# Second mamba layer: first half batch loaded during the 1-bit layer before it, the residual's moments taken between the scans

## The reference, cut to what matters

```python
# second 1-bit layer
x = x + linear_bit(silu(linear_bit(x_n, w1, g1)) * linear_bit(x_n, w2, g2), w3, g3)
# second mamba layer: hidden_states = ctx_1024 (4, 512, 256), z = layernorm(x)
xi = einsum('bld,ed->bel', hidden_states, in_proj_w)          # (4, 512, 512)
u = silu(conv1d(xi, conv_w, 4 taps, per channel) + conv_b)
dt_low, B, C = split(einsum('bdl,ed->bel', u, x_proj_w))      # 16 + 16 + 16 rows
delta = softplus(dt_low @ dt_proj_w + dt_proj_b)
A = -exp(A_log)                                               # (512, 16)
state_t = exp(delta_t * A) * state_(t-1) + delta_t * u_t * B_t
y_t = sum over the 16 states of state_t * C_t
x = x + swap((y + D * u) * silu(z))
```

## Time and profile before

| | us |
|---|---|
| median of 3 runs | 4210.7 (4209.96 to 4212.67) |
| the profiled execution | 4212.01 |
| its span | 4210.3 |

### The profile page before, as it was taken

One profiled execution on the slowest core, in us unless ns is written; L12 is line 12 of the kernel. 1 busy time (PEld: TensorE's weight loads), 2 busy tenths in 40 slices (PEclk: granted clock), 3 DMA queues, 4 the chain that ended last, 5 costly groups with the idle time before them and its releaser, 6 DMA issues. The chain is left out here.

```text
span 4210.3 us, 47286 instructions
## 1 busy us (share of the span) xinstructions
PE 3635.0 (86%) x15355; PEld 1743.4 (41%) x15355; DVE 2959.2 (70%) x4185; ACT 1801.8 (43%) x3009; POOL 1463.2 (35%) x1046
## 2 busy tenths in 40 slices
PE   6889865999999999898999879785876888689898
PEld 2333333555555555542333344333332333244454
DVE  3999988578777884457888266527667999834663
ACT  3655541222222221243777453327664655421244
POOL 1889854122211220063000100004436999800122
PEclk8999987999999999997999989896998999989999
DMA  3455441122233212266774110001005555412420
GB/s 104 128 149 141 128 136 54 49 85 69 80 100 100 80 32 72 114 152 97 78 78 47 53 60 0 3 9 64 0 0 141 139 137 138 131 39 70 79 55 22
DMA packets 249834, 338.37 MB, mean 80 GB/s; under 512 B 45602, under 2 KB 147522, under 8 KB 248036
## 3 DMA queue, kind: packets, MB, share of 16 engines
q1 hardware_dynamic: 249620, 335.70, 32.1%
HBM read 284.38 MB, written 53.35 MB: 80 GB/s over the span
## 5 line engine op out<-in xcount | busy, mean ns | idle before, releaser
L727 ACT ACTIVATE m_dA<-m_delta,m_a_neg 128x512 f32<-128x512 f32 x512 | 349.8, 690 | 411.1 <-DVE m_H_bank L806 344.2
L566 PE MATMUL m_y<-m_H,ident 128*128 128x512 f32 x512 | 283.3, 641 | 150.0 <-DVE m_H L823 149.6
L1913 DVE TENSOR_REDUCE a_core_minus_max<-a_core_a 128x1 f32<-128x512 f32 x512 | 317.1, 684 | 59.9 <-PE a_core_a L1739 59.9
L747 POOL TENSOR_TENSOR m_dB<-m_du,m_BC 128x1024 f32<-128x1024 f32 x128 | 302.0, 2360 | 123.0 <-DVE m_du L786 84.5
L736 POOL TENSOR_TENSOR m_H<-m_H,m_BC 128x512 f32<-128x512 f32 x240 | 306.7, 1278 | 95.8 <-DVE m_H L815 95.4
L747 POOL TENSOR_TENSOR XN<-m_du,m_BC 128x1024 f32<-128x1024 f32 x128 | 305.9, 2390 | 2.6 <-DMA m_BC<-bc_ready 2.6
L1865 ACT ACTIVATE X<-a_core_s 128x512 f32<-128x512 f32 x512 | 264.6, 603 | 95.3 <-PE a_core_s L1739 95.2
L1305 POOL TENSOR_TENSOR ctxT<-ctxT,f_scales 128x1024 f32<-128x1024 f32 x48 | 107.0, 2229 | 532.3 <-DVE ctxT L1130 532.3
L574 PE MATMUL m_y<-m_H,ident 128*128 128x512 f32 x512 | 268.4, 612 | 12.0 <-POOL m_H L736 11.9
L1265 ACT ACTIVATE XN<-f_g,f_power_back 128x512 f32<-128x512 f32 x128 | 88.0, 687 | 404.3 <-PE f_g L1202 404.3
L1371 DVE SCALAR_TENSOR_TENSOR XN<-f_u,f_power_back,XN 128x512 f32<-128x512 f32 x128 | 95.8, 748 | 227.9 <-PE f_u L1202 227.9
(11 more groups left out here) (416 smaller groups left out, 8461.5 us busy)
## 6 DMA issues: line engine op xcount, KB each, us to landing
m_BC<-bc_rows SPq DMA_DIRECT2D x224, 512.0 KB, 4.8
XN<-in_L_ffn_w_dram SPq DMA_DIRECT2D x72, 256.0 KB, 2.7
m_BC<-bc_ready SPq DMA_DIRECT2D x32, 512.0 KB, 4.8
ternary<-ctxT SPq DMA_DIRECT2D x96, 128.0 KB, 1.7
a_core_q<-a_q_parts SPq DMA_DIRECT2D x48, 256.0 KB, 12.8
a_core_k<-a_k_parts SPq DMA_DIRECT2D x48, 256.0 KB, 14.8
f_w_tern<-ternary SPq DMA_DIRECT2D x24, 512.0 KB, 6.0
f_core_q<-f_q_parts SPq DMA_DIRECT2D x24, 512.0 KB, 7.9
```

Of the source, the lines that this page charges most:

```text
L566: pe.matmul(ps_y[:, 0, :], ident[:], HD[n % NH], start=False, stop=True, skip_group_check=True).then_inc(s_ad, 1)
L727: act.activation(dA[:, i % NA, :], delta[b % 2][:, e, :], ACT.Exp, scale=a_neg[:, e, k % N:k % N + 1]).then_inc(s_dA, 1)
L747: pool.tensor_tensor(dB[n % ND][:], du[b % 2][:, h * EH:(h + 1) * EH, :], BC[n % NS][:, 0:1, :].broadcast_to([P, EH, L]), ALU.mult).then_i ...
L1913: dve.tensor_reduce(mx[u % 2][:, qt, h:h + 1], ps_a[:, at % NR, 0:n], AX.X, ALU.max, negate=True).then_inc(s_red, 1)
```

## The change

- A new class `FirstHalf` holds delta and du of the first half batch, the first B row and A_log in tiles of their own, allocated before the 1-bit layer, and loads them in that layer's token loop, right behind the issue of the third gain row.
- The second mamba layer's SP queue now begins with BC 0 to 3 and u, then the five small transfers, the weight rows, BC 4 and the second halves. ScalarE waits for the early transfers (`s_half`) instead of the small ones. GpSimd takes the first B row from the early tile. VectorE's wait for the small transfers, and what follows it up to the raised counts, stay as they are.
- The 16 statistics go to steps 4 to 11, two to a step, the aggregates to step 12, root and inverse to step 13, the first batch's gates to steps 15 and 17. The tap diagonals go to steps 1 to 4.
- delta and du become tiles by half. The projection weights are loaded into a part of XN, and the ternary slots lie where xqT comes later, which makes the room.

```diff
+        elif spare is not None:
+            self.in_rows = spare[:, 1:3, :].rearrange("p t (two c) -> p (t two) c", two=2)
+            self.x_rows, self.dt_rows = spare[0:self.W, 0, :], sb("dt_rows", [P, self.EB, self.R])
...
+class FirstHalf:
+    def __init__(self, chip, name, st, parked, bc_parked, a_log, half):
+        self.parked, self.bc_parked, self.a_log, self.half = parked, bc_parked, a_log, half
+        self.delta, self.du = (chip.sb(f"{name}_early_{n}", [P, half, L], F32, st) for n in ("delta", "du"))
+        self.B = chip.sb(name + "_early_B", [P, 1, L], F32, st)
+        self.a_in = chip.sb(name + "_early_a", [P, 2 * half, a_log.shape[1]], F32, st)
+        self.s_half = chip.sem(name + "_early")
+    def load(self, sp):
+        sp.dma_start(self.a_in[:], self.a_log.rearrange("(e p) c -> p e c", p=P)).then_inc(self.s_half, 16)
+        for i, out in ((1, self.delta), (2, self.du)):
+            sp.dma_start(out[:], self.parked[i][:, 0:self.half, :]).then_inc(self.s_half, 16)
+        sp.dma_start(self.B[:], self.bc_parked[0:1].rearrange("(o n) t -> n o t", o=1).broadcast_to([P, 1, L])
+                     ).then_inc(self.s_half, 16)
...
-        ROOT, INVERSE = 5, 7
+        DIAGONAL, MOMENT, ROOT, INVERSE, GATES = 1, 4, 13, 13, (15, 17)
...
-        DIAGONALS = {(0, 3 + e): e for e in range(EB)} if given else ...
+        DIAGONALS = {(0, DIAGONAL + e): e for e in range(EB)} if given else ...
...
             if given:
+                for k in range(NS - 1):
+                    rows_of(0, k)
+                sp.dma_start(u[0][:, 0:EH, :], parked[0][:, 0:EH, :]).then_inc(s_gu, 16)
                 weights.load_small(sp)
-                for i in (2, 1):
-                    park_or_load(i, 0)
-                for k in range(2):
-                    rows_of(0, k)
-                park_or_load(0, 0)
                 weights.load_rows(sp)
-                for k in range(2, NS):
-                    rows_of(0, k)
-                for i in (2, 1, 0):
-                    park_or_load(i, 1)
+                rows_of(0, NS - 1)
+                for out, i in ((du, 2), (delta, 1)):
+                    sp.dma_start(out[0][1][:], parked[i][:, EH:EB, :]).then_inc(s_given, 16)
+                sp.dma_start(u[0][:, EH:EB, :], parked[0][:, EH:EB, :]).then_inc(s_gu, 16)
...
-            act.wait_ge(weights.s_small, weights.SMALL)
+            if given:
+                act.wait_ge(given.s_half, 64)
+            else:
+                act.wait_ge(weights.s_small, weights.SMALL)
...
-                    if k in SILU:
-                        gates(b, SILU.index(k))
+                    if k in (GATES if b < FIRST else SILU):
+                        gates(b, (GATES if b < FIRST else SILU).index(k))
...
                     pool.wait_ge(s_du, b * EB + (h + 1) * EH)
                     if b < FIRST and k % N == 0:
-                        pool.wait_ge(s_given[h], 32)
-                    pool.wait_ge(s_bc[n % NS], 16 * (n // NS + 1))
+                        pool.wait_ge(s_given if h else given.s_half, 32 if h else 64)
+                    if n >= FIRST:
+                        pool.wait_ge(s_bc[n % NS], 16 * (n // NS + 1))
...
+                    row = given.B[:] if n < FIRST else BC[n % NS][:, 0:1, :]
...
             dve.wait_ge(s_pad, 2)
-            norm.moments(dve)
+            if given:
+                norm.begin(dve)
+            else:
+                norm.moments(dve)
...
-                    if given and b == 0 and k == INVERSE:
+                    if b < FIRST and MOMENT <= k < MOMENT + NT // 2:
+                        norm.moment(dve, 2 * (k - MOMENT))
+                        norm.moment(dve, 2 * (k - MOMENT) + 1)
+                    if b < FIRST and k == MOMENT + NT // 2:
+                        norm.aggregate(dve)
+                    if b < FIRST and k == INVERSE:
                         norm.inverse(dve)
...
-        tern = [sb(f"tern{n}", [P, 4, 512], BF16) for n in range(SLOTS)]
+        flat = [at[:].rearrange("p t k n -> p (t k n)") for at in xqT]
+        tern = [at[:, i * 2048:(i + 1) * 2048].rearrange("p (j k) -> p j k", j=4) for at in flat for i in range(4)]
+        tern += [sb(f"tern{n}", [P, 4, 512], BF16)[:] for n in range(len(tern), SLOTS)]
...
             if gains:
                 sp.dma_start(g3, gains[2].rearrange("(o n) -> o n", o=1).broadcast_to([P, F])).then_inc(s_g3, 16)
+            ahead(sp)
+            if gains:
                 sp.wait_ge(s_g3, 16)
...
         with ExitStack() as held:
-            chip.run(stage_mamba, "m3", bc, ScanWeights(chip, "m3", held, *mamba_args(a, "L3")),
-                     given=(ready, bc_ready))
+            early = FirstHalf(chip, "m3", held, ready, bc_ready, a["L3_xattn_A_log"], 2)
+            chip.run(stage_bitffn, "f2", signs[3:6], 3, [a["L2_ffn_g" + n] for n in "123"], ahead=early.load)
+            chip.run(stage_mamba, "m3", bc, ScanWeights(chip, "m3", held, *mamba_args(a, "L3"),
+                                                           spare=chip.XN[:, 3 * TB:4 * TB, :]), given=early)
```

More of the change, by code:

```diff
@@ L321, in stage_mamba, with tiles, tile @@
         xdbl, positive = sb("xdbl", [W, L]), XN[:, 3 * TB:4 * TB, :]
-        u, delta, du = ([sb(f"{n}{i}", [P, EB, L]) for i in range(2)] for n in ("u", "delta", "du"))
+        u = [sb(f"u{i}", [P, EB, L]) for i in range(2)]
+        delta, du = ([[at if given else sb(n + "0", [P, EH, L]), sb(n + "0_second", [P, EH, L])]] for n, at in (
+            ("delta", given and given.delta), ("du", given and given.du)))
+        for x, n in ((delta, "delta"), (du, "du")):
+            x.append([sb(f"{n}1_{h}", [P, EH, L]) for h in range(2)])
+        def tiles(x, b, e, count):
+            return x[b % 2][e // EH][:, e % EH:e % EH + count, :]
+        def tile(x, b, e):
+            return x[b % 2][e // EH][:, e % EH, :]
         NH, NA, ND = 4, 3, 4
@@ L348, in stage_mamba @@
         s_wg, s_wgc, s_diag, s_park = sem("reweigh"), sem("reweigh_copied"), sem("diagonals"), sem("parked")
-        s_given, s_gu = [sem(f"given{h}") for h in range(2)], sem("given_u")
+        s_given, s_gu = sem("given_second"), sem("given_u")
         s_a, s_skip, s_pad = sem("a"), sem("skip"), sem("padded")
@@ L367, in stage_mamba @@
         LAG, TIMES_U, COPY_SUM = 3, 2, 4
-        ROOT, INVERSE = 5, 7
+        DIAGONAL, MOMENT, ROOT, INVERSE, GATES = 1, 4, 13, 13, (15, 17)
         REWEIGH = {(0, 1): (0, 1), (0, 2): (2, 3)} if given else {(2, k): (i,) for i, k in enumerate((20, 21, 22, 25))} if then else {}
         REWEIGH_LAG = 1 if given else 3
-        DIAGONALS = {(0, 3 + e): e for e in range(EB)} if given else {(2, 20 + e): e for e in range(EB)} if then else {}
+        DIAGONALS = {(0, DIAGONAL + e): e for e in range(EB)} if given else {(2, 20 + e): e for e in range(EB)} if then else {}
         def project_at(b):
@@ L409, in _, with park @@
         def _(sp):
[L410 to L416, removed]
+            def park(i, h):
+                rows = slice(h * EH, (h + 1) * EH)
+                here = tiles((delta, du)[i - 1], B, h * EH, EH) if i else u[0][:, rows, :]
+                sp.dma_start(parked[i][:, rows, :], here).then_inc(s_park, 16)
             def rows_of(b, k):
@@ L543, in work @@
                     pe.wait_ge(s_err, 2 * b + i // EH + 1)
-                    pe.matmul(out, ident[:], delta[b % 2][:, i, :], start=True, stop=False)
-                    pe.matmul(out, ident[:], du[b % 2][:, i, :], start=False, stop=False)
+                    pe.matmul(out, ident[:], tile(delta, b, i), start=True, stop=False)
+                    pe.matmul(out, ident[:], tile(du, b, i), start=False, stop=False)
                     pe.matmul(out, ident[:], positive[:, i, :], start=False, stop=True).then_inc(s_sum, 1)
@@ L659, in step @@
                     act.wait_ge(s_sum, b * EB)
-                act.activation(delta[b % 2][:, e, :], bank("step", b, e), ACT.Abs,
+                act.activation(tile(delta, b, e), bank("step", b, e), ACT.Abs,
                                bias=small(b)[:, e, TAPS + 1:TAPS + 2]).then_inc(s_ab, 1)
@@ L668, in exp_part @@
                 act.wait_ge(s_conv, (b + 1) * EB)
-                act.activation(xin[:, rows, TAPS - 1:], delta[b % 2][:, rows, :], ACT.Exp, scale=-1.0).then_inc(s_e, 1)
+                act.activation(xin[:, rows, TAPS - 1:], tiles(delta, b, h * EH, EH), ACT.Exp, scale=-1.0).then_inc(s_e, 1)
             def log_part(b, h):
@@ L673, in log_part @@
                 act.wait_ge(s_e, 2 * b + h + 1)
-                act.activation(delta[b % 2][:, rows, :], xin[:, rows, TAPS - 1:], ACT.Ln, bias=1.0).then_inc(s_ln, 1)
+                act.activation(tiles(delta, b, h * EH, EH), xin[:, rows, TAPS - 1:], ACT.Ln, bias=1.0).then_inc(s_ln, 1)
             def copy_sum(b, e):
@@ L678, in copy_sum @@
                 act.wait_ge(s_du, b * EB + e + 1)
-                act.copy(delta[b % 2][:, e, :], bank("sum", b, e)).then_inc(s_del, 1)
```

(7 more changed lines are left out.)

37 lines of the change are left out of this document (21 added, 16 removed).

## The result

The changed kernel takes 4223.26 us (median of 9 runs, 4220.58 to 4228.86) against 4210.82 of before (9 runs, 4209.96 to 4215.51). The ratio is 1.0027, 95% interval 1.0019 to 1.0036: slower by 12.4 us, 8.0 to 15.2. Forecast were +5.5 us and 4208 to 4222, so it is slower than the forecast and 1.3 us outside the range. (12.4 is the difference of the two medians; 8.0 to 15.2 are the bounds of the ratio, in us.)

The account below looks back on a forecast made before the run. DMA waits, then VectorE's moments, were taken to bound the first scan, and VectorE the first batch. Terms +0.7 + 7.5 + 1.0 - 2.4 - 1.3 = +5.5 us gave 4217.5, forecast as 4216.2 us (median-based); range 4208 to 4222.

Parts of the forecast that it names:

- Term 1: Start of the second mamba layer: small loads moved back put the first scan at 3186.9, +0.7 us (-5.4 to +3.5).
- Term 3: Tap diagonals moved from steps 3 to 6 to steps 1 to 4: +1.0 us (0 to +3).
- everything else: Ternary slots, weight rows in XN, tiles split in halves: only addresses change, no instruction's size, 0 us.
- rival D: SP stalls on a full queue, the last small load lands late at 3186.3: +9.6 us, 4220.3 us, chance 0.21.
- Rival B: Small loads land by their issue, at 3177.3, making the first scan earlier: 4210.1 us, chance 0.13.
- Terms 2 to 4: Between the scans: moments in the loop +7.5 us, tap diagonals +1.0, root, inverse and gates -2.4.
- Term 5: First log error at step 22: GpSimd runs out sooner, shortening its first instruction's wait, -1.3 us (-2.6 to 0).
- a log error far from 4 us: Sign at step 22 that would show the log error's forecast of -1.3 us wrong.
- C: GpSimd's 3.54 us a step is the pace, so moments only fill VectorE's idle time: +1.7 us, 4212.4, chance 0.10.

Follow-up runs that it names:

- second pair: Both kernels, before and changed, run and profiled once more unchanged; whole layer 509.99 us before and 517.46 us after.
- Experiment 2: Changed kernel, with VectorE waiting for its four skip diagonals before raising the counts that release GpSimd; 4222.66 us, ratio 1.0021 to before.
- Experiment 1: Changed kernel with the five small transfers first in SP's queue again, ahead of the B/C pairs and u; 4212.46 us, ratio 0.9999 to before.
- experiment 4: Changed kernel with all statistics and aggregates taken before VectorE's wait for the small loads, none between the scans; 4218.33 us, ratio 1.0007 to before.
- experiment 3: Changed kernel with the small loads also issued in the 1-bit layer's loop, A_log loaded once; 4209.71 us, ratio 0.9988 to before.
- experiment 6: experiment 3 with all 16 tap diagonals made beside the skip diagonals, ahead of the increments releasing GpSimd; 4205.53 us, ratio 0.9985 to before.
- experiment 10: experiment 6 with weight rows behind the first two B/C pairs, u last, statistics in steps 2 to 9, aggregates in 10; 4201.34 us, ratio 0.9968 to before.
- experiment 11: The changed kernel run once more, unchanged, for a second profile; 4224.19 us.

## Why the prediction was wrong

- **Term 1, the first scan: predicted +0.7 us, measured +5.4 (+5.5 in the second pair). This is the step that failed.** Its first half held: the small loads were predicted at 14.0 us after the start and landed at 14.7. What failed is "Behind it come four diagonals (0.28 us each, one every 0.22, so 0.9), a semaphore (0.1), and the product (2.35)". They do not come one after the other. The count is raised while three diagonals are pending, GpSimd starts beside them, and the diagonals take 7.34 us; from the landing to the first scan it is 7.28 us instead of 3.4, 3.9 too much. I had used that very effect for the tap diagonals and not for these four, because the earlier trace rows show them in a kernel where GpSimd was still waiting for its B row. Taking that wait away took the diagonals' cover away. Experiment 2, where they do come one after the other, has 3.54 us there.
- **Term 3, the tap diagonals: predicted +1.0, measured -1.4.** It is the other side of the same mistake: GpSimd runs through its products during the skip diagonals, so that step 1 takes 6.37 us and not 8.75. In experiment 2 it takes 8.29. The failed step thus costs 3.9 us in term 1 and gives some 2 of them back here; settling the diagonals gained 0.7 to 1.8 us in all.
- **The whole up to step 22: predicted +5.5, measured +9.3 (+9.5).** The 3.8 us between them are +0.7 for the landing, +3.9 for the skip diagonals, -2.4 for term 3 and +1.5 for step 12 to 13. With +9.3 alone the time would have been about 4220, inside the range. What took it out of the range are 3 us more, of which the point on "everything else" speaks.
- **What makes the first scan late at all was named rightly: the order of the queue.** Experiment 1 takes 10.4 to 12.6 us off the layer by that order alone. The trace agrees with the rule of the Trainium skill ("DMA: Bandwidth & Descriptors", section "Queues, rings and completion order") that each DMA engine consumes its ring in order and that the write to the semaphore lands only after that engine's earlier writes: the last small transfer reported at 14.7 us, u, issued ahead of it, at 13.1. (The five small transfers raise one semaphore, so the landings of the first four can't be told apart.) But the trace does not show that the rings held it up, since its wait lay in SP. The five issues took 0.96, 1.35, 1.89, 1.25 and 2.96 us instead of 0.4 to 1.0; the last ended 13.0 us after the start, and the transfer landed 1.73 us behind that, as it did in before with no large transfer ahead of it (1.77). It was 1.73, 1.72 and 1.79 in the second profile and in experiments 2 and 4. This is rival D's mechanism. D's time did not come: the last transfer was to land at 16.8 us, and from 15.6 on D was to decide. Whether it would have landed earlier if SP had not stalled, no run shows. Rival B, a landing at 7.8 us, is out.
- **Terms 2 to 4, between the scans: predicted +6.1 us to step 21, measured +5.2 (+5.3).** Steps of 4.0 us, as said. Moments and the stall of step 10 together were +4.35 and came out as +4.3, but my split was wrong: I credited the stall's end to the gates' leaving; without the moments it is 4.45 us even with the gates gone (experiment 4). Step 12 to 13 took 6.44 us and not 4.9: ScalarE's root waits 2.1 us for the aggregates, which I did not price. Steps 15 and 17 stall 0.84 and 0.52 us (0.5 and 0.7 forecast). That the sum comes within 1 us is luck in part, since the error of term 3 and that of step 13 have opposite signs.
- **Term 5: -1.3 us, measured -1.3** (step 21 to 22 took 9.17 us instead of 10.46). The log error's first instruction took 5.16 us instead of 6.44. The term was the middle of two bounds, and the same instruction took 0.68 to 5.18 us in the experiments, so this hit is luck too. The sign "a log error far from 4 us" does not fit the term either, by which it should have been 5.1.
- **"Everything else 0": open, with more for it than against.** The layers differ by 8.5 us on average of two profiles, the medians by 12.4, whose interval reaches down to 8.0. The span less the layer was 3700.2 and 3701.8 us in before, 3705.0 and 3707.5 in after, but also 3708.2, 3706.7, 3703.3, 3699.1 and 3700.6 in experiments 2, 3, 1, 6 and 10, which share after's edits to the other stages. It moves by 9 us from run to run without following the edit. The other experiments say more: in the nine that share these edits, the difference of the medians from before on the same chip, less the difference of the layers, is -2.5 to +1.5 us, 0.3 on average. So a cost of 3 to 4 us outside the layer is not seen again. The kernel before had its lowest median in just this pair, 4210.8 against 4213.5 to 4215.1 beside the experiments, and after's single time in experiment 11, 4224.19, is 9.1 us above before's median there, with a layer 7.4 us longer. That points to scatter of the pair, but one time is too little to settle it.
- **The rivals.** C (GpSimd's pace makes the moments free) is refuted by steps of 4.01 us. D, forecast at +9.6, was nearest in size and right about SP's stall; most of its price came by another way, 7.3 us of diagonals in place of a landing at 16.8 us. The upper end of the range was given as +11.3; the terms named for it add up to +10.6.

## What to carry to other kernels

When a wait is removed, look at the first use of every transfer that it let stand first in the queue: here 2.5 MB were put ahead of five transfers of 2 to 32 KB that gate everything, and that cost 10 to 13 us of the layer, where the early load won 4 to 8. When an engine is released earlier, ask which instructions of its neighbour had been free only because it stood idle. And a count raised by an instruction of its own behind some others in a queue does not say that they are done: here three of four, and in experiment 6 ten of twenty, had not started.

## What the runs showed of the hardware that was not expected

- A 128x128 f32 tensor_scalar takes 0.28 us with GpSimd idle. Beside a GpSimd that works without a pause it takes up to 2.5 us, and ends some 0.1 us behind the GpSimd instruction that it met. The statistics (0.68 us) and the scans (1.2 us) take the same time with and without it.
- The wait can be longer than one instruction: the first 128x1024 tensor_scalar of the log error took 6.44, 5.16, 1.8 and 0.68 us in before, after and experiments 1 and 6. What decides it was not settled.
- SP's issue instruction itself grows from 0.5 us to 1 to 3 us with 2.5 MB and small transfers outstanding (of the small transfers' issues 3.67 at most, in experiment 4), and the last small transfer landed 1.7 to 1.8 us behind the end of its issue with and without them. Which amount outstanding decides was not measured.
